# Gathers of 128 row numbers on tiles of 125 edges, and one near tile fewer in three of the five phases

## What is computed

```
L0: h = relu(edge_attr16 @ W1 + b1); w = (h @ W2 + b2) -> 16x16 for each edge
    msg = x[src] . w ; sum by dst ; + x @ root + bias ; batch norm ; relu
L1: m = silu(sum_ij x[dst]_i * edge_attr8_j * W_msg[i,j,:]) ; sum by src ; @ W_lin ; gated update
L2: msg = x[src] @ W[type] / count[dst, type] ; sum by dst ; + x @ root + b   (twice) ; log_softmax
L3: x[src] * outdeg^-0.5 ; sum by dst ; * indeg^-0.5
```

## Time and profile before

| | |
|---|---|
| median of 2 runs | 4555.14 us |
| the profiled execution | 4555.6 us, of which span 4553.4 us |
| TensorE, its weight loads | 95%, 72% of the span busy |
| VectorE | 91% |
| ScalarE | 71% |
| GpSimd | 72% |
| mean granted TensorE clock | 0.983 of full speed |
| indirect gathers | 2500 (l0 800, l1 500, l2a 400, l2b 400, l3 400) |

### The profile page before, as it was taken

How to read it: one execution, slowest core, us unless ns; L and a number is a source line. 1 busy time by engine, 2 the same in 40 slices (tenths; PEclk the granted TensorE clock), 3 DMA queues, 4 the chain that set the end, 5 groups by cost and what they waited for, 6 DMA issues and landing times.

```text
span 4553.4 us, 107759 instructions
## 1 busy us (share of the span) xinstructions
PE 4339.6 (95%) x30477; PEld 3261.8 (72%) x30477; DVE 4121.4 (91%) x11864; ACT 3235.6 (71%) x5359; POOL 3284.9 (72%) x2515
## 2 busy tenths in 40 slices
PE   4999999999997999999979999998999999799998
PEld 3777777777775777777747777776777777566665
DVE  5999999999997999999969999997999998888887
ACT  3777777777774777777737777775777777677776
POOL 4888888888883777777727777775777775688886
PEclk8999999999998999999989999999999999899999
DMA  3111111111111222222211111111111111111111
GB/s 72 21 17 18 17 18 17 18 18 18 18 17 40 61 59 61 59 60 60 59 37 27 27 28 27 27 28 39 27 28 28 26 28 23 30 31 31 30 31 24
DMA packets 336556, 148.67 MB, mean 33 GB/s; under 512 B 250040, under 2 KB 322532, under 8 KB 336392
## 3 DMA queue, kind: packets, MB, share of 16 engines
q0 software_dynamic: 104000, 59.31, 10.1%
q1 hardware_dynamic: 232517, 88.88, 7.8%
HBM read 135.45 MB, written 9.80 MB: 32 GB/s over the span
## 4 chain that ended last, share of the span: by engine, by line
PE 81%; DVE 10%; issue 5%; ACT 2%; DMA 1%; SPq 1%; DVEq 0%; POOL 0%; POOLq 0%; ACTq 0%
PE acc L600 37%; PE rows_ps L757 16%; PE rows_ps L693 7%; PE bank L773 5%; PE bank L693 4%; PE counts L607 3%; PE eaT_ps L765 3%; DVE raw L1258 2%; PE rows_ps L681 2%; DVE stationary L1234 2%; PE eaT_ps L669 1%; DVE one_hot L1206 1%; PE counts L604 1%; DVE rows_ps L1321 1%; ACT stack L928 1%
## 5 line engine op out<-in xcount | busy, mean ns | idle before, releaser
L600 PE MATMUL acc<-one_hot,stationary 125*128 125x392 bf16 x12000 | 2335.4, 329 | 39.5 <-DVE stationary L1234 35.1
L584 POOL DMA_INDIRECT gathered<-table_l,row_numbers x1200 | 1607.3, 1339 | 461.1 <-issue 349.1
L600 PEld LDWEIGHTS acc<-one_hot,stationary 125*128 125x128 bf16 x12000 | 1157.3, 100 | 709.0 <-DVE stationary L1234 49.9
L866 ACT ACTIVATE distances<-count_hi,fields 125x392 bf16<-125x392 f16 (+1 forms) x2500 | 1227.5, 560 | 0.0
L1234 DVE TENSOR_TENSOR stationary<-mask,parts 125x1024 bf16<-125x1024 bf16 x1500 | 943.3, 683 | 0.3 <-ACT mask L851 0.2
L851 ACT CAST mask<-is_lo 125x1024 bf16<-125x1024 f32 x500 | 523.1, 1046 | 447.3 <-DVE is_lo L1187 393.5
L584 POOL DMA_INDIRECT fields_all<-table_l,row_numbers x500 | 646.3, 1293 | 259.6 <-issue 114.8
L1206 DVE TENSOR_SCALAR one_hot<-count_hi,fields 125x392 bf16<-125x392 f16 x2300 | 734.4, 341 | 13.5 <-issue 13.5
L1321 DVE COPY_PREDICATED rows_ps<-near_bits_now,rows_ps 125x320 f32<-125x320 int8 (+3 forms) x1600 | 579.7, 362 | 162.6 <-PE rows_ps L757 118.6
L584 POOL DMA_INDIRECT gathered<-table_l2a,row_numbers x400 | 512.7, 1282 | 282.6 <-DVE parts L1216 119.4
L757 PE MATMUL rows_ps<-node_parts,h1T 125*125 125x192 bf16 (+1 forms) x7200 | 678.3, 252 | 27.0 <-DVE node_parts L1285 19.6
(11 more groups left out here) (213 smaller groups left out, 4706.6 us busy)
## 6 DMA issues: line engine op xcount, KB each, us to landing
near_key<-near_keys_by_chunk SPq DMA_DIRECT2D x300, 122.1 KB
gathered<-table_l,row_numbers POOLq DMA_INDIRECT x1200, 2.8
fields<-edge_fields SPq DMA_DIRECT2D x500, 31.2 KB
near_key<-near_keys_by_chunk SPq DMA_DIRECT2D x100, 91.6 KB
fields_all<-table_l,row_numbers POOLq DMA_INDIRECT x500, 3.5
gathered<-table_l2a,row_numbers POOLq DMA_INDIRECT x400
gathered<-table_l2b,row_numbers POOLq DMA_INDIRECT x400
ea<-in_edge_attr SPq DMA_DIRECT2D x100, 62.5 KB
```

The costliest lines, as they stand in the source:

```text
L584: pool.indirect_dma_start(out=gathered[ph][:, s, t, :], in_=table[ph], out_offset=None, in_offset=bass.IndirectOffsetOnAxis(ap=row_numbers ...
L600: mm = pe.matmul(acc[:, :], stationary[:, s, k, t, :, :].rearrange("p a b -> p (a b)"), one_hot[:, s, t, :], start=first and t == 0 and k ...
L866: ins = act.activation(distances[:, i * n:(i + 1) * n], count_hi[:, 0:n], ACT.Abs, scale=-1.0, bias=fields[:, s, k, t:t + 1].bitcast(F32))
```

## The change

The tiles stay at 125 edges. The tile of row numbers and the tiles that gathers write have 128 partitions in place of 125. The row numbers are cleared to 0 once at the start by GpSimd, SyncE loads 125 partitions of them as before, and the indirect DMA of line 584 of before, whose own text is unchanged, now covers 128 partitions: rows 125 to 127 of each gather fetch table row 0 and nobody reads them. In l1 one near tile becomes a far one (3 to 2), in l2a and l2b one each (4 to 3). l0 (none) and l3 (4) keep theirs.

```diff
 EP, T = 125, 8
+ROWS = 128
...
-NEAR_OF = {"l0": (0, 0), "l1": (3, 3), "l2a": (4, 4), "l2b": (4, 4), "l3": (4, 4)}
+NEAR_OF = {"l0": (0, 0), "l1": (2, 2), "l2a": (3, 3), "l2b": (3, 3), "l3": (4, 4)}
...
-        fields_all = sb("fields_all", [EP, CHUNKS, FIELDS, T], I32)
-
-        reused = fields_all[:].rearrange("p c k t -> p (c k t)").bitcast(F32)
+        all_fields = sb("fields_all", [ROWS, CHUNKS, FIELDS, T], I32)
+        fields_all = all_fields[0:EP]
+
+        reused_rows = all_fields[:].rearrange("p c k t -> p (c k t)").bitcast(F32)
+        reused = reused_rows[0:EP]
...
-        row_numbers = sb("row_numbers", [EP, 2, T], I32)
+        row_numbers = sb("row_numbers", [ROWS, 2, T], I32)
...
-        gathered0 = sb("gathered0", [EP, 2, T, 2 * F])
-        gathered1 = reuse(2, T, RELATIONS * F + RELATIONS)
-        gathered2 = sb("gathered2", [EP, 2, T, F])
+        rows0 = sb("gathered0", [ROWS, 2, T, 2 * F])
+        gathered0 = rows0[0:EP]
+        rows1 = reuse(2, T, RELATIONS * F + RELATIONS, room=reused_rows)
+        gathered1 = rows1[0:EP]
+        rows2 = sb("gathered2", [ROWS, 2, T, F])
+        gathered2 = rows2[0:EP]
...
-        gathered = {"l0": gathered0, "l1": gathered1, "l2a": gathered2, "l2b": gathered2, "l3": gathered2}
+        gathered = {"l0": rows0, "l1": rows1, "l2a": rows2, "l2b": rows2, "l3": rows2}
...
-                sp.dma_start(row_numbers[:, s, :], rows.rearrange("p c n -> p (c n)")).then_inc(numbers_in[s], 16)
+                sp.dma_start(row_numbers[0:EP, s, :], rows.rearrange("p c n -> p (c n)")).then_inc(numbers_in[s], 16)
...
         @block.gpsimd
         def _(pool):
+            pool.memset(row_numbers[:].rearrange("p s t -> p (s t)"), 0)
             pool.memset(x[:], 0.0).then_inc(ev("x_cleared"), 1)
```

More of the change, by code:

```diff
@@ L144, in build, with reuse @@
         src, dst, typ, work, work2 = (room[:, i * TILES:(i + 1) * TILES].bitcast(I32) for i in range(5))
-        fields_all = sb("fields_all", [EP, CHUNKS, FIELDS, T], I32)
-        reused = fields_all[:].rearrange("p c k t -> p (c k t)").bitcast(F32)
+        all_fields = sb("fields_all", [ROWS, CHUNKS, FIELDS, T], I32)
+        fields_all = all_fields[0:EP]
+        reused_rows = all_fields[:].rearrange("p c k t -> p (c k t)").bitcast(F32)
+        reused = reused_rows[0:EP]
         used = [0]
-        def reuse(*shape):
+        def reuse(*shape, room=reused):
             size = int(np.prod(shape))
@@ L154, in reuse @@
             names = " ".join("abcd"[:len(shape)])
-            return reused[:, at:at + size].rearrange(f"p ({names}) -> p {names}", **dict(zip("abcd", shape)))
-        row_numbers = sb("row_numbers", [EP, 2, T], I32)
+            return room[:, at:at + size].rearrange(f"p ({names}) -> p {names}", **dict(zip("abcd", shape)))
+        row_numbers = sb("row_numbers", [ROWS, 2, T], I32)
         fields = sb("fields", [EP, 2, FIELDS, T], I32)
```

## The result

The changed kernel takes **4356.41 us** (median of 2 runs, 4354.89 and 4357.93), 0.9566 of before, 95% interval 0.9543 to 0.9589. Forecast were 4355 us. Everything ahead of e8 was measured where the change pays: the result itself, and e1 to e4 on a device on which before takes 4553.17 us.

What follows compares the result with a forecast made beforehand. The prediction took TensorE to bound l1 and l2 before the change and VectorE after it. Gains of 44 us in l1, 138 in l2a and l2b and 18 in l3 made 200 of 4555.6, so 4355 us, range 4280 to 4540.

Steps and rivals of the forecast that it cites:

- part 1: Near tiles on TensorE: 1.06 us each in l1, 0.82 in l2; TensorE's limits fall to 7.43 and 6.44 us a chunk.
- part 2: Near tiles on VectorE: busy 7.78 and 6.35 us a chunk; at 96.6% busy, limits of 8.05 (l1) and 6.57 us (l2).
- rival 3: TensorE stays the bound in l1 and l2, at 7.43 and 6.44 us a chunk: 4255 us, chance 0.13.
- g: Undisturbed time of one gather on GpSimd: 1.205 us before, taken as 0.93 with 128 rows, bounds 0.39 to 1.205.
- part 3: Gathers on GpSimd: one more a chunk in l1 and l2, each cheaper; GpSimd needs 7.82 and 6.46 us, barely below VectorE.
- a third of the way down: Choice of 0.93 us for a 128-row gather, between the upper bound 1.205 and the lower 0.39.
- The collisions: Extra gather time on GpSimd from collisions with VectorE's work, left at 0.44 us a chunk in l1 and 0.31 in l2.
- part 4: l3 and l0, counts unchanged: cheaper gathers hold up VectorE less, gaining 18 us in l3 (0 to 30), 0 in l0.
- The sum: Whole kernel: gains of 44 us in l1, 138 in l2a and l2b, 18 in l3, together 200, giving 4355 us.
- Rival 1: The gather stays at 1.205 us and GpSimd bounds l1 and l2, at 9.47 and 7.84 us: 4770 us, chance 0.19.

Runs made afterwards that it cites:

- e8: The kernel after, unedited, run on another device: 5684.62 us, 1.2349 of before, which takes 4586.13 us there.
- e1: The kernel after with the near tiles of before (3, 4, 4), so only the gathers of 128 rows: 4523.23 us, ratio 0.9933.
- e4: e1 with gathers of 112, 96, 64, 32 and 16 row numbers in l0, l1, l2a, l2b and l3: 4525.46 us.
- e3: e1 with gathers of 126, 128, 127, 125 and 128 row numbers in l0, l1, l2a, l2b and l3: 4945.02 us.
- e2: The kernel before with the near tiles of after (2, 3, 3), gathers of 125 rows kept: 4794.94 us, ratio 1.0531.
- e5: The kernel after with one gather fewer a chunk in l1, l2a and l2b, on the device of e8: 5105.94 us, 1.1125.
- e9: The kernel after with gathers of 125 rows in l0 and l3, 128 elsewhere, on the device of e8: 5256.58 us, 1.1464.

## Why the prediction was right

**The near tile's price and TensorE's bound** (part 1). e1 keeps l1 at 847.4 us with TensorE at 100%. With one near tile fewer, it leaves the chain. Right.

**VectorE next** (part 2). Right for l1, and for l2 in part. Its busy time a chunk in l1 is 659.37 / 700 x 8.31 = 7.83 us (forecast 7.78), in l2a 583.05 / 600 x 6.49 = 6.31 (6.35). The share that it can reach was 97.2% in l2a and 94.2% in l1, where 96.6% was assumed for both. That is the mis-sized term: l1 saved 18 us in place of 44. l2a came out at 6.49 and l2b at 6.57 on average, where 6.57 was forecast. But in l2 TensorE is level with VectorE. Its own limit was put at 6.44 us (part 1). l2a, at 6.49 with TensorE busy for 599.56 of 600 us, lies within 1% of it, and the first third of l2b, at 6.39, is on it. That is the mark which the prediction had set for rival 3. VectorE is seen to hold up both other engines only in the later part of l2b (6.68 us).

**g** (part 3). 0.942 us for 0.93. The choice of a third of the way down had no row behind it, and it was luck that it fell so near. What the trace of before did give was the 400 elements against 128. That elements cost time, 13 to 15.5 ns for each that an engine gets, only e3 and e4 showed. The Trainium skill (DMA: Bandwidth & Descriptors, Why a DMA increments its semaphore by 16) has the rule of the divisor. The packets of 125 and of 128 rows and the bytes and the 2542 ns of 127 rows agree with it. The same page's remark that many descriptors can be emitted before their cost shows does not hold here: 17 elements an engine more cost 0.26 us of 1.205.

**The collisions** (part 3) were held at 0.44 us a chunk in l1. They are now 6 x (1.079 - 0.942) = 0.82 us, so GpSimd needs 6 x (1.079 + 0.305) = 8.30 us, just the period, and in l2a 5 x (0.993 + 0.305) = 6.49, again the period. It has no pause in either, where small ones were forecast. Does it bound them? A missing pause does not show it: in l0 before it had none either, and start and l0 together fell by only 12 us when GpSimd was freed of more than 2 us a chunk. The time at which rows are read says more. Of l1 in e2, then of l1 in the kernel after:

```profile
DVE fields_all L1434 <- DMA fields_all<-table_l,row_numbers: 36.0, 31, 1.5
...
1762.32 0.94 POOL L591 DMA_INDIRECT fields_all<-table_l,row_numbers  x1 [0.30 <-issue]
...
1767.39 0.96 DVE L1441 TENSOR_TENSOR fields_all<-fields_all,ea 125x768 f32<-125x768 f32 x1 [0.27 <-issue]
```

Counted by six from l1's first gather, the gather at 1762.32 is the last of a chunk, and the product at 1767.39 is the first to read that chunk's rows, 4.1 us after the gather's end. From the 20th chunk on the distance is 3.7 to 4.1 us without any drift, where e2, in which VectorE waits for rows, has 2.2 to 2.7. In l2a it is 4.9 to 5.3 us against 1.4 to 1.7. So VectorE is not kept waiting for rows, which speaks against GpSimd as the bound, and in l1 it waits for nobody else that the profile names. How much the gathers stretch VectorE's own instructions, and why both engines come out at one period, is not shown, since e5 met the stalls.

**l3 and l0** (part 4). 22.6 us in place of 18, and 12 from the start on in place of 0. Right in kind: GpSimd's hold on VectorE eased. In 4000:4300, before and after:

```profile
L1206 DVE TENSOR_SCALAR one_hot<-count_hi,fields 125x392 bf16<-125x392 f16 x188 | 60.8, 365 | 7.0 <-issue 7.0
L1213 DVE TENSOR_SCALAR one_hot<-count_hi,fields 125x392 bf16<-125x392 f16 x196 | 57.3, 334 | 7.0 <-issue 7.0
```

Four one-hots a chunk are 0.12 us shorter together, about half of what a chunk gained (6.43 to 6.20 us, counted by four gathers). The other half is not traced.

**The sum.** That it came within 1.4 us was luck. l1 was put 26 us too high, and l2, l3, the start with l0 and the time between the phases were 5, 5, 12 and 2 us too low.

**Rival 1** was the fork that mattered. e2 gives 4795 us where its sum gave 4770, l1 at 9.56 (9.47) and l2a at 7.93 (7.84). The prediction did not see that the same gathers could stall the engines on another device, and nothing in the trace of before could have told it.

## What to carry to other kernels

Where a producer runs beside the bound, look up what sets its unit cost before moving work to it: here three useless rows cut a gather by 22% and so made room for one more in each chunk, and neither edit was worth much, or anything, alone. Count the packets of one transfer against the rows that it should move, as fillers give the spread away. Time such a change on more than one device before it is kept.

## What the runs showed of the hardware

- A gather costs GpSimd about 0.83 us plus 13 to 15.5 ns for each element of the DMA engine that gets most, with the engines the largest divisor up to 16 of the row count: 127 rows cost 2.54 us, 128 cost 0.94.
- A count that is not spread over all 16 costs a little more than its elements say: 120 rows (15 x 8) 978 ns on the third device beside 942 for 128 (16 x 8).
- VectorE's bf16 one-hots are held up by a gather in progress (0.32 to 1.07 us beside 2.5 us gathers), its f32 product and its selections from PSUM and its bf16 product of two tiles are not. The Trainium skill (SBUF — State Buffer, SBUF: two separate sides) describes a port pair of VectorE and GpSimd that one of them locks. These rows agree.
- On two of the three devices that the experiments met, gathers of 0.90 to 1.0 us come with stalls of VectorE and ScalarE, 3.9 us on average and up to 11.7 in e8. All 466 of e8 wait for TensorE, whose semaphores rise 1.5 to 11.4 us after the recorded end of a matmul, where the first device has 0.02 us at most and e9's l0, with gathers of 125 rows, 0.15. With the stalls in all phases the kernels ran 21 to 25% slower than before. Gathers of 1.2 us bring two short ones (e9's l3) or none. Why TensorE is late is not shown.
